# A two-layer graph attention kernel: the adjacency read in two 1 MB transfers per row tile, and the row stages with one normalization per step

## What is computed

```python
# layer 0: graph attention (GAT), scores are a product of two per-node numbers
x_l = (x @ W + b).reshape(N, 8, 64)
scores = alpha_l[:, None, :] * alpha_r[None, :, :]
scores = where(adj[:, :, None] > 0, scores, NEG_INF)
out = einsum('ijh,jhc->ihc', softmax(scores, axis=1), x_l)
x = layernorm(x + relu(out))
# layer 1: dot-product attention, q = x, k = x2, masked by the same adj
scores = where(adj > 0, einsum('hnd,hmd->hnm', q * 64 ** -0.5, k), NEG_FILL)
out = einsum('hnm,hmd->hnd', softmax(scores, axis=-1), v)
x = layernorm(x + out)
```

## Time and profile before

| | us |
|---|---|
| median of 3 runs (3721.36 to 3723.89) | 3721.69 |
| the profiled execution | 3723.63 |
| its span, first to last instruction | 3721.7 |
| `prepare`, about 0 to 360 of the span | 360 |
| `attend_gat`, about 360 to 1650 | 1290 |
| `finish_layer` of layer 0, about 1650 to 1804 | 154 |
| `attend_dot`, about 1804 to 3619 | 1815 |
| `finish_layer` of layer 1, about 3619 to 3722 | 103 |

### The profile page before, as it was taken

How to read it: one execution, slowest core, us unless ns; L and a number is a source line. 1 busy time by engine, 2 the same in 40 slices (tenths; PEclk the granted TensorE clock), 3 DMA queues, 4 the chain that set the end, 5 groups by cost and what they waited for, 6 DMA issues and landing times. The chain is left out here.

```text
span 3721.7 us, 57866 instructions
## 1 busy us (share of the span) xinstructions
PE 3514.0 (94%) x22311; PEld 1411.8 (38%) x22311; DVE 2925.2 (79%) x2984; ACT 2527.6 (68%) x2430; POOL 1535.2 (41%) x1154
## 2 busy tenths in 40 slices
PE   6886999999999999987699999999999999999987
PEld 4554222222222222235244444444444444444434
DVE  6666999999999999977577777777777777777768
ACT  4555999999999999953466566666666666666642
POOL 2222011011011011010277776777766667766761
PEclk9988999999999999985799999999999999999995
DMA  8987677777767777667799999999999999999987
GB/s 282 312 303 252 154 155 158 155 157 167 162 156 157 158 155 165 149 162 244 174 200 198 203 205 201 203 203 199 202 205 204 200 199 201 204 204 201 196 188 246
DMA packets 370652, 729.38 MB, mean 196 GB/s; under 512 B 26672, under 2 KB 215088, under 8 KB 354016
## 3 DMA queue, kind: packets, MB, share of 16 engines
q0 software_dynamic: 99408, 419.90, 58.1%
q1 hardware_dynamic: 236944, 272.23, 23.8%
q10 hardware_dynamic: 34048, 33.82, 2.7%
HBM read 263.50 MB, written 59.69 MB: 87 GB/s over the span
## 5 line engine op out<-in xcount | busy, mean ns | idle before, releaser
L1131 DVE TENSOR_TENSOR a_weights<-a_psS,maskT 128x1024 f32<-128x1024 f32 x1024 | 1206.0, 1220 | 465.5 <-ACT a_psS L1095 465.4
L1095 ACT ACTIVATE a_psS<-a_psS,shift_bc 128x1024 f32<-128x1024 f32 x1024 | 1071.4, 1084 | 678.8 <-PE a_psS L1023 678.7
L541 DVE TENSOR_TENSOR g_weights<-g_weights,maskT 128x1024 f32<-128x1024 f32 x1024 | 1169.8, 1219 | 116.6 <-ACT g_weights L528 116.6
L528 ACT ACTIVATE g_weights<-al_bc,shift_bc,g_xl 128x1024 f32<-128x1024 f32 x1024 | 1167.9, 1228 | 88.0 <-PE g_psD L566 88.0
L1023 PE MATMUL a_psS<-a_q,a_k 128*64 128x512 f16 x8192 | 971.3, 380 | 18.9 <-DMA a_k<-k_scratch 17.2
L1040 PE MATMUL a_psO<-a_weights,a_v 128*64 128x512 f32 x4096 | 961.2, 592 | 0.0
L557 PE MATMUL g_psO<-g_weights,g_xl 128*64 128x512 f32 x4096 | 923.6, 598 | 14.3 <-DVE g_weights L541 14.3
L1154 POOL TENSOR_TENSOR a_pool_total<-a_pool_total,a_weights 128x1024 f32<-128x1024 f32 x336 | 924.8, 2753 | 0.0
L1023 PEld LDWEIGHTS a_psS<-a_q,a_k 128*64 128x64 f16 x8192 | 463.3, 110 | 648.7 <-issue 318.9
L1162 POOL DMA_DIRECT2D a_dma_total<-a_weights x480 | 466.2, 971 | 398.8 <-DVE a_weights L1131 207.8
L557 PEld LDWEIGHTS g_psO<-g_weights,g_xl 128*64 128x64 f32 x4096 | 277.8, 137 | 651.2 <-issue 521.6
(11 more groups left out here) (122 smaller groups left out, 1373.2 us busy)
## 6 DMA issues: line engine op xcount, KB each, us to landing
a_dma_total<-a_weights POOLq DMA_DIRECT2D x512, 512.0 KB, 5.4
g_total<-g_weights POOLq DMA_DIRECT2D x128, 1024.0 KB, 7.8
adj_sb<-in_adj_dram SPq DMA_DIRECT2D x128, 512.0 KB, 6.0
g_xl<-xl_scratch SPq DMA_DIRECT2D x128, 260.0 KB, 5.6
a_k<-k_scratch SPq DMA_DIRECT2D x256, 128.0 KB, 5.4
a_v<-in_L_gnn_v_dram SPq DMA_DIRECT2D x128, 256.0 KB, 4.0
al_bc<-alpha_scratch SPq DMA_DIRECT2D x16, 1024.0 KB, 7.1
f_oT<-o_scratch SPq DMA_DIRECT2D x16, 1024.0 KB, 7.5
```

What stands on the lines that cost most here:

```text
L528: nc.scalar.activation(w[:, u % RING, h, :], al_bc[:, g % 2, h, :], ACT.Exp, bias=shift_bc[:, 0, g % PAIRS * 2 + h:g % PAIRS * 2 + h + 1], ...
L541: nc.vector.tensor_tensor(w[:, u % RING, h, :], w[:, u % RING, h, :], maskT[:, j, (g // PAIRS) * IC:(g // PAIRS + 1) * IC], ALU.mult).then ...
L1095: nc.scalar.activation(psS[n % RING][:], psS[n % RING][:], ACT.Exp, bias=shift_bc[:, 1, g % PAIRS * 2 + h:g % PAIRS * 2 + h + 1], scale=SC ...
L1131: nc.vector.tensor_tensor(w[:, u % NP, h, :], psS[n % RING][:].rearrange("p a c -> p (a c)"), maskT[:, j, (g // PAIRS) * IC:(g // PAIRS + ...
```

## The change

Three edits in `prepare`, and five in `finish_layer` (both calls).

- `prepare`: two transfers of 1 MB per row tile, each for two banks, each issued when DVE has compared both of its banks; two semaphores `adj_loaded` instead of four. The compares stay four.
- `normalize` takes a tile instead of a round: in step t ACT normalizes tile t - 4. The round's 1 MB store follows its fourth tile. In the last round each tile has its own store of 256 KB, which waits for that tile.
- `qh` and `ql` have QB = 3 buffers instead of 2.
- The denominators' turn is issued as a transpose (`is_transpose=True`), as L724's already are.
- `finish_layer` of layer 1 runs NT + 4 steps instead of NT + 1.

```diff
-                    for bank in range(4):
-                        sp.wait_ge(compared[bank], t)
-                        sp.dma_start(adj_sb[:, bank, :], adj[rows, bank * QN:(bank + 1) * QN]
-                                     ).then_inc(adj_loaded[bank], 16)
+                    for half in range(2):
+                        for bank in (2 * half, 2 * half + 1):
+                            sp.wait_ge(compared[bank], t)
+                        sp.dma_start(adj_sb[:, 2 * half:2 * half + 2, :].rearrange("p b n -> p (b n)"),
+                                     adj[rows, 2 * half * QN:2 * (half + 1) * QN]).then_inc(adj_loaded[half], 16)
...
-                        dve.wait_ge(adj_loaded[bank], t * 16 + 16)
+                        dve.wait_ge(adj_loaded[bank // 2], t * 16 + 16)
...
-        STEPS = NT + LAG if first else NT + 1
+        STEPS = NT + LAG if first else NT + T
...
-                nc.tensor.matmul(psR[t % 2][:], dT[0:H, par, cols], identF[0:H, 0:H], start=True, stop=False)
+                nc.tensor.matmul(psR[t % 2][:], dT[0:H, par, cols], identF[0:H, 0:H], is_transpose=True, start=True,
+                                 stop=False, skip_group_check=True)
...
-            def normalize(r):
-                act.wait_ge(rstd_ready, r + 1)
-                act.wait_ge(offset_ready, r + 1)
-                for s in range(T):
-                    nc.scalar.activation(z[:, r % ZB, s, :], z[:, r % ZB, s, :], ACT.Identity,
-                                         bias=offset[:, r % 2, s:s + 1], scale=rstd[:, r % 2, s:s + 1]
-                                         ).then_inc(res_ready, 1)
-                act.wait_ge(res_ready, T * (r + 1))
-                act.dma_start(result[r * T * P:(r + 1) * T * P, :].rearrange("(t p) c -> p t c", p=P),
-                              z[:, r % ZB, :, :]).then_inc(res_stored[r % ZB], 16)
+            def normalize(t):
+                r, s = divmod(t, T)
+                if s == 0:
+                    act.wait_ge(rstd_ready, r + 1)
+                    act.wait_ge(offset_ready, r + 1)
+                nc.scalar.activation(z[:, r % ZB, s, :], z[:, r % ZB, s, :], ACT.Identity,
+                                     bias=offset[:, r % 2, s:s + 1], scale=rstd[:, r % 2, s:s + 1]
+                                     ).then_inc(res_ready, 1)
+                if r == R - 1:
+                    act.wait_ge(res_ready, t + 1)
+                    act.dma_start(result[t * P:(t + 1) * P, :], z[:, r % ZB, s, :]).then_inc(res_stored[r % ZB], 16)
+                elif s == T - 1:
+                    act.wait_ge(res_ready, t + 1)
+                    act.dma_start(result[r * T * P:(r + 1) * T * P, :].rearrange("(t p) c -> p t c", p=P),
+                                  z[:, r % ZB, :, :]).then_inc(res_stored[r % ZB], 16)
...
             for t in range(STEPS):
-                if t > 0 and t % T == 0 and t <= NT:
-                    normalize(t // T - 1)
+                if T <= t < NT + T:
+                    normalize(t - T)
```

More of the change, by code:

```diff
@@ L159, in prepare @@
         wa_ready = sem("wa_ready")
-        adj_loaded = [sem(f"adj_loaded{i}") for i in range(4)]
+        adj_loaded = [sem(f"adj_loaded{i}") for i in range(2)]
         x_loaded = [sem(f"x_loaded{i}") for i in range(2)]
@@ L629, in finish_layer @@
         LAG = 7
+        QB = 3
         PARTS = (0, 32, 64)
@@ L670, in finish_layer @@
         if first:
-            qh = sb("qh", [P, 2, PAIRS, 2 * P], F16)
-            ql = sb("ql", [P, 2, PAIRS, 2 * P], F16)
+            qh = sb("qh", [P, QB, PAIRS, 2 * P], F16)
+            ql = sb("ql", [P, QB, PAIRS, 2 * P], F16)
             v_sum = sb("v_sum", [P, F], F32)
@@ L680, in finish_layer @@
             v_loaded = sem("v_loaded")
-            q_stored = [sem(f"q_stored{i}") for i in range(2)]
+            q_stored = [sem(f"q_stored{i}") for i in range(QB)]
             tail = sem("tail")
         block = ctx.enter_context(nc.Block())
-        STEPS = NT + LAG if first else NT + 1
+        STEPS = NT + LAG if first else NT + T
         @block.sync
@@ L729, in turn @@
                     pe.wait_ge(inverted, t - 1)
-                nc.tensor.matmul(psR[t % 2][:], dT[0:H, par, cols], identF[0:H, 0:H], start=True, stop=False)
-                nc.tensor.matmul(psR[t % 2][:], alone[:, par, cols], times_n[:], start=False, stop=True
-                                 ).then_inc(turned, 1)
+                nc.tensor.matmul(psR[t % 2][:], dT[0:H, par, cols], identF[0:H, 0:H], is_transpose=True, start=True,
+                                 stop=False, skip_group_check=True)
+                nc.tensor.matmul(psR[t % 2][:], alone[:, par, cols], times_n[:], start=False, stop=True,
+                                 skip_group_check=True).then_inc(turned, 1)
             def turn_queries(t):
@@ L775, in upper @@
                 act.wait_ge(q_turned, t + 1)
-                if half == 0 and pair >= 2:
-                    act.wait_ge(q_stored[pair % 2], 32 * (pair // 2))
-                nc.scalar.activation(qh[:, pair % 2, :, half * P:(half + 1) * P], psQ[t % 3][:], ACT.Copy
+                if half == 0 and pair >= QB:
+                    act.wait_ge(q_stored[pair % QB], 32 * (pair // QB))
+                nc.scalar.activation(qh[:, pair % QB, :, half * P:(half + 1) * P], psQ[t % 3][:], ACT.Copy
                                      ).then_inc(qh_ready, 1)
@@ L784, in store_queries @@
                     act.dma_start(q_dram[part].rearrange("(a p) n -> p a n", p=P)[:, :, pair * 2 * P:(pair + 1) * 2 * P],
-                                  qq[:, pair % 2, :, :]).then_inc(q_stored[pair % 2], 16)
+                                  qq[:, pair % QB, :, :]).then_inc(q_stored[pair % QB], 16)
             act.wait_ge(consts_set, 1)
             for t in range(STEPS):
-                if t > 0 and t % T == 0 and t <= NT:
-                    normalize(t // T - 1)
+                if T <= t < NT + T:
+                    normalize(t - T)
                 if t < NT and t % T == T - 1:
@@ L798, in _ @@
                 store_queries(NT // 2 - 1)
-                for i in range(2):
-                    act.wait_ge(q_stored[i], 32 * (NT // 4))
+                for pair in range(NT // 2 - QB, NT // 2):
+                    act.wait_ge(q_stored[pair % QB], 32 * (pair // QB + 1))
             for r in range(R - ZB, R):
-                act.wait_ge(res_stored[r % ZB], 16 * (r // ZB + 1))
+                act.wait_ge(res_stored[r % ZB], 16 * (r // ZB + (T if r == R - 1 else 1)))
         @block.gpsimd
@@ L882, in lower @@
                 dve.wait_ge(qh_ready, t + 1)
-                if half == 0 and pair >= 2:
-                    dve.wait_ge(q_stored[pair % 2], 32 * (pair // 2))
-                nc.vector.tensor_tensor(ql[:, pair % 2, :, cols], psQ[t % 3][:], qh[:, pair % 2, :, cols],
+                if half == 0 and pair >= QB:
+                    dve.wait_ge(q_stored[pair % QB], 32 * (pair // QB))
+                nc.vector.tensor_tensor(ql[:, pair % QB, :, cols], psQ[t % 3][:], qh[:, pair % QB, :, cols],
                                         ALU.subtract).then_inc(ql_ready, 1)
```

## The result

| | before | after |
|---|---|---|
| median, us | 3721.98 (3721.36 to 3724.12, 6 runs) | 3701.56 (3700.89 to 3704.19, 6 runs) |
| ratio | | 0.9945, 95% interval 0.9932 to 0.9958 |
| profiled execution; its span | 3723.63; 3721.7 | 3700.89; 3699.3 |

The kernel is 20.4 us faster; 18 had been forecast, from the row stages alone. Its trace says the same of the place. First the stretches: length, then busy time with instructions of PE, PEld, DVE, ACT and POOL, then TensorE clock, DMA share, GB/s.

What follows compares the result with a forecast made beforehand. DVE, stalled by ACT, was taken to pace layer 0's row stage; in `prepare` the compare-product loop, not the loads. Terms 15.8 + 1.5 + 0.5 + 0.3 + 0 = 18.1 us gave 3704, range 3695 to 3719.

Steps and rivals of the forecast that it cites:

- Rounds of layer 0: Layer 0's row stage, rounds 1 to 7: DVE's 2.36 us stall goes, the 0.85 stays; 15.8 us gained, bounds 15.0 and 17.
- The tail of layer 0: Last round's normalization to the last query store's issue in layer 0: 15.9 us becomes 13.7; 1.5 taken, bounds 0 and 2.2.
- The turn: Denominators' turn loses one of two passes, felt only at each layer's first tile: 0.5 us for both layers, bounds 0 and 0.8.
- The end of layer 1: Layer 1's last round: last issue 1.6 us later, landing 2.0 us shorter; 0.3 us gained, bounds -1 and +1.
- The loads: Adjacency loads in `prepare`: first half lands in 5.4 us, under 5.66 allowed, so 0; bounds 44 us lost and 6 gained.
- One of the signs that were to prove the prediction wrong: In `prepare`: 1 MB landing later than 5.7 us after its issue would show the prediction wrong.
- rival 1: Layer 0's row stage: the stall moves instead of going, two stalls of 0.85 a round, costing 5 us: 3709; chance 0.12.
- rival 2: `prepare`: the first half of the adjacency load lands late, each 1 us over 5.66 costing 24 us, up to 3748; chance 0.20.
- rival 3: `prepare`: the adjacency loads were the bound and larger transfers free them, worth 6.1 us: 3698; chance 0.05.
- rival 4: The row stages do nothing: DVE is as late as before for an unseen reason, and 3720 stays; chance 0.03.

Runs made afterwards that it cites:

- one last store: The changed kernel with the last round stored in one transfer of 1 MB again, in both layers: 3702.8 us, ratio 0.9947 to the kernel before.
- square late: The changed kernel with POOL's square of x2 waiting for the tile's last compare: 3712.7 us, ratio 0.9966 to the kernel before.

## Why the prediction was right, and where its sizes were off

- **Rounds of layer 0.** Forecast 15.8 us over six rounds, with bounds of 15 and 17; measured 16.84. The mechanism is as argued: the 2.4 us stall at t % 4 == 0 is gone and the 0.85 stays, once a round. Five rounds are 13.57 to 13.69 apart and the last 12.83, 13.5 in the mean where 13.7 was forecast; the last was the shortest before too (15.32). DVE's waits of `ql` fell from 20.9 to 5.1, the 15.8 to the tenth. They were not all pairs of 0.85 and 2.36, as the one round shown had it: 14.0 of the 15.8 are the second stall, and 1.9 is what the first was over 0.85 in four rounds, which the third buffer removed, as the prediction had said of its waits. The extra microsecond lies beside them. A `DVE f_z` that waited for `offset` no longer does, 0.5 us:

```profile
DVE f_z L867 <- DVE f_offset L851: 0.5, 1, 0.5
```

  (this row is of before, 1685 to 1784). And a `ql` that has nothing to wait for starts 0.09 us before the instruction ahead of it ends (1712.97, with the aggregation ahead of it, 1712.88, until 1713.06), which six more of them do now: another 0.5.
- **The tail of layer 0.** Forecast 1.5, at most 2.2; measured 2.9: from `offset` at 1765.03 to the last query store's issue at 1777.73 are 12.70 us, before 15.61. This is the term that was mis-sized, and its upper bound was wrong. The sum of ACT's work gave 13.7 us from the first normalization to the end of the last issue; it took 13.0 (1765.29 to 1778.26). I had charged 0.91 us of ACT's time for each pair of query stores, 2.7 for three. The rows of after show less for the first pair:

```profile
1768.33 0.60 ACT L786 ACTIVATE f_qh<-f_psQ 128x512 f16<-128x512 f32 x1 [0.49 <-ACT f_z L770]
1768.36 0.38 ACTq L792 DMA_DIRECT2D q_scratch<-f_qh  x1
1768.77 0.58 ACTq L792 DMA_DIRECT2D q_scratch<-f_ql  x1
1769.40 0.81 ACT L770 ACTIVATE f_z<-f_z,f_offset,f_rstd 128x512 f32<-128x512 f32 x1 [0.47 <-issue]
```

  Both issues begin while ACT's own `qh` still runs (until 1768.93), and ACT stands still for 0.47 us and not 0.91. Behind the next two pairs it stands still for 0.63 and 1.24 us (waiting for PE and for `ql`), 2.3 in all, so this accounts for 0.4 of the 0.7 us; the rest is spread over instructions that begin about 0.1 us before the one ahead of them ends. The other 0.7 of the miss is the discount from 2.2 to 1.5, taken for waits for PE that came to little. The prediction also gave no cause to the gain: it didn't name ACT's 4.1 us of waits for a query store in the tail of before, and the third buffer alone brings 2.4 of the 2.9 us.
- **The turn.** Forecast 0.5 for both layers; the trace has 0.3 at layer 0's first tile, and the run without it shows no difference.
- **The end of layer 1.** Forecast 0.3 with bounds of -1 and +1. From `offset` (3691.96) to the end of the span (3699.3) are 7.3 us, before 8.0 (3713.72 to 3721.7): 0.6. The last issue comes 4.81 us after `offset` and lands in 2.0; before, 3.22 after it, and 4.3. Issuing thus cost the 1.6 forecast, and the landing gave back 2.3 and not 2.0:

```profile
3696.77 0.34 ACTq L775 DMA_DIRECT2D out_dram<-f_z  x1
...
out_dram<-f_z ACTq DMA_DIRECT2D x1, 256.0 KB, 2.0
```

  The trace with one last store has the 8.0 again; its median, 1.2 us above after, proves nothing.
- **The loads.** Forecast 0, on a landing of 5.4 against 5.66 allowed; measured 5.0 to 5.1 against 5.73 where it is tight, and no wait. The exposure was counted too large: two tiles of a round are tight and not three, 16 and not 24, so by the same count a microsecond over would have cost 16 us and not 24. One of the signs that were to prove the prediction wrong was badly put: 1 MB did land later than 5.7 us after its issue, 6.6 in the median of the 48 halves between 60 and 300, but those that did have room, and nothing waited. Two readings beside this were off. The compares other than the second are not 0.76 us each but 1.16, 0.68 and 0.68. And without POOL's square the half is issued 1.2 us earlier (1.97 us into the tile at 209.32 with the square late, against 3.13), not 1.6. The Trainium skill (DMA: Bandwidth & Descriptors, Anatomy of one DMA) would give 4.4 us for 1 MB, though for transfers issued from GpSimd; the measured ones decide, and they are 0.6 to 0.7 us longer.
- **The rivals.** The stall did not move (rival 1): one 0.85 a round, and none in the next step. The first half was not late (rival 2), by 0.6 us. The loads were not the bound (rival 3): a third less was moved (205 GB/s against 309) and nothing was gained. The row stages did shorten (rival 4).

The terms of the trace are 16.8 + 2.9 + 0.6 = 20.3 us, and the medians differ by 20.4. The two spans differ by 22.4; the other 1.9 us stands ahead of round 0 of layer 0's row stage (`offset` at 1674.10 and 1672.20), of which 0.3 is the turn; the rest is no more than the variation of the stages ahead, and the profiled execution of after is the fastest of its six. That the three terms meet the difference of the medians to 0.1 us is luck: either median is good to a microsecond or so.

## What to carry to other kernels

Find the engine that sets the pace and list its waits by their place in the loop: here a stall that came twice a round, in two sizes, gave the gain of the rounds within 7%, while a DMA share of 0.84 in `prepare` pointed at an edit worth nothing. A tile whose store hasn't landed is a full buffer: when you speed up a loop, ask which buffer the faster pace will find full, and give it a second one in the same edit, because each of the two edits may show nothing, or a loss, by itself. When an edit shows nothing, look in its trace for a wait that went and another that came. Differences of a few microseconds between single traces need a run with the suspected part left as it was.

## What the runs showed of the hardware that was not expected

- A store's landing moves with the loads around it: `k_scratch<-kl`, 512 KB, took 5.9 us in the median in after, 4.7 with half the bytes loaded (205 GB/s against 309), and 14.4 with the square late, when the mid-round tiles were 7% faster, though the mean rate of the stretch was no higher (290 GB/s). What it queues behind is not shown.
- It works the other way too: a 1 MB load of SP's issued 2.1 to 2.7 us behind a pair of 256 KB stores of ACT's landed in 6.3 to 7.8 us, seven times of seven, and in 5.0 to 5.1 without them.
- One compare of 128x1024 beside a GpSimd square of 1.05 us costs about 1.15 us more than without it (four of them 4.12 and 2.96).
- Two transfers that ACT began to issue while its own instruction still ran cost it 0.47 us, and not the sum of their 0.38 and 0.58.
